# Four rounds of a graph network: the order of the stages in two softmax loops

## The chip, the cores and the metric

One core of one Trainium2 chip runs the kernel. The time is that of the device, in microseconds, for one execution: the kernel before takes 10075.73 us (median of 3 runs, 10074.14 to 10075.74). A smaller number is better. The profile comes from one execution, whose span is 10045.6 us.

## The reference

Four rounds work on 12500 nodes with 64 features and 212500 edges, sorted by the node they end in (`dst`). Each normalises the nodes, sends something along the edges, sums per `dst` and adds the result to the nodes. The change touches the first and the fourth, which both take a softmax over the edges that end in one node:

```python
# round 0 (for each of the 64 features on its own)
m = relu(feats[src] + edge_h) + EPS
gmax = segment_max(m, dst)
ex = exp(m - gmax[dst])
den = segment_sum(ex, dst)
h = segment_sum(m * ex / den[dst], dst)
# round 3 (4 heads of 16 features, 8 relations)
s = leaky_relu(el_all[edge_rel, src] + er_all[edge_rel, dst], 0.2)
m = segment_max(s, dst)
e = exp(s - m[dst])
denom = segment_sum(e, dst)
agg = segment_sum(feat_all[edge_rel, src] * e / denom[dst], dst)
```

Round 1 is a mean over the edges, round 2 a hyperbolic attention. They stay as they are.

## The kernel before, in words

The four edge loops run one after the other, each followed by a part that works on nodes: `softmax_edges(0)` takes about 230 to 2390 us of the span and `softmax_edges(3)` about 7710 to 9880 us.

`softmax_edges` cuts the sorted edges into two halves that are worked on side by side, each half on 64 of the 128 partitions, and takes 512 edges (`W`) of each half in a step: 208 steps (`STEPS`). In a step the edges lie along the free dimension, so the maximum and the sums of a segment can be made by scans along it, which carry their last column on from step to step. Instead of an exponential against the final maximum, the scans use the maximum so far, and the factor `ps_ex` by which the sums so far have to shrink. A step passes through these stages; the letters in brackets are used later:

- GpSimd gathers the rows of `src` by 8 indirect DMAs (L649) into one of four buffers (`SLOTS`). It waits (`rows_read`, the same counter as `turned`) until TensorE has read the step four back.
- SyncE loads the segment marks `part_b` and, for layer 0, the edge attributes, for layer 3 the rows `v_e` and `marks`, also four buffers deep.
- Layer 0: `to_columns` (TensorE, L764 and L766) turns rows and attributes into `ps_score` and adds them; `move` (ScalarE, L824) is the relu. `put_in_bins` (VectorE, L667) and `count` (TensorE, L752) are a histogram that later rounds want; they need nothing of the gathered rows.
- Layer 3: `v_columns` (TensorE, L775) turns `v_e`, `own_values` (VectorE, L676 and L681; OV) makes `own_v` from it, `widen` (ScalarE, L813) spreads the gathered scores over the 16 features of a head, `score_columns` (TensorE, L781 reads `own_v`, L784 reads `wide`, L788 turns the gathered features; SC) makes the scores, `move` (ScalarE, L822; M) copies them.
- `maxima` (VectorE, L688 in layer 3 only, L695, L699, L704, L705, L707; MX): the running maximum and the two differences.
- `exps` (ScalarE, L828 and L829; EX): both exponentials, and the DMA of the maxima (L830).
- `segment_sums` (VectorE, L713, L716, L719; SS): the weighted values and the two running sums.
- `to_rows` (TensorE, L796; TR) turns the sums back, `copy_out` (ScalarE, L836) copies them out of PSUM, `store` (ScalarE's queue, L844) writes them by two DMAs.

Each engine runs its instructions in the order written. That order comes from `written_out`: it is given pairs of a lag and a stage, and for s = 0, 1, 2, ... emits, in the order of the list, each stage for step s minus its lag. Semaphores between the engines are counted per step, so any stage waits until its own inputs are there; `ex`, `weighted`, `ps_ex` and (layer 3) `score_c` exist once, the running `top` and `sums` and `own_v` twice, `ps_score` twice in layer 3 and three times in layer 0.

Of the kernel before, what the change touches and what calls it, by code (L numbers as in the profile page):

```python
# [65 lines left out]
STEPS = CHUNKS // HALVES  # L66
# [10 lines left out]
def build(nc, x, src, dst, edge_attr, edge_type, w0a, b0a, gamma, beta, w0b, b0b, scale0,  # L77
          w1, b1, w2, c2, w3, al3, ar3, b3, out):
    with ExitStack() as whole:
# [448 lines left out]
        def written_out(n, *stages):  # L528

            for s in range(n + max(lag for lag, _ in stages)):  # L530
                for lag, stage in stages:
                    if 0 <= s - lag < n:
                        stage(s - lag, (s - lag) % SLOTS, (s - lag) // SLOTS)

        def softmax_edges(layer):
# [7 lines left out]
            with nc.cleanup_on_exit(), ExitStack() as ctx:  # L543
# [51 lines left out]
                with nc.Block() as block:  # L595
# [60 lines left out]
                    def _(dve):  # L656
# [63 lines left out]
                                                 initial=sums[:, 1 - q, 1, W - 1:W], op0=ALU.mult, op1=ALU.add).then_inc(summed, 1)  # L720

                        if rel:
                            written_out(STEPS, (0, own_values), (3, segment_sums), (2, maxima))
                        else:
                            written_out(STEPS, (0, put_in_bins), (2, segment_sums), (1, maxima))

                        step = stepper(dve, m_step)
                        top_a = top[0:D, END, W:W + 1]
# [17 lines left out]
                    @block.tensor  # L746
                    def _(pe):
                        def count(c, b, r):
                            pe.wait_ge(binned, c + 1)
                            pe.sem_inc(pe_turn, 1)  # L750
                            for t in range(2):
                                mm = nc.tensor.matmul(ps_count[:, t, 0:HOT], ident_b[:, :],  # L752
                                                      hot[:, b % 2, t, :, :].rearrange("p j b -> p (j b)"),
                                                      start=isinstance(c, int) and c == 0,
                                                      stop=isinstance(c, int) and c == STEPS - 1)
                            mm.then_inc(counted, 1)

                        def to_columns(c, b, r):
                            pe.wait_ge(got_edge[b], r * 32 + 32)
                            slot_free(pe, weighed, c, ago=SCORES)  # L760
                            pe.wait_ge(got_rows[b], r * ROWS + ROWS)
                            pe.sem_inc(pe_turn, 1)
                            for k in range(TILES):
                                nc.tensor.matmul(ps_score[:, c % SCORES, k::TILES], rows[:, b, k, :], ident[:, :], start=True, stop=False)  # L764
                                for h in range(HALVES):
                                    mm = nc.tensor.matmul(ps_score[h * D:(h + 1) * D, c % SCORES, k::TILES], attr[:, b, h, k, :],  # L766
                                                          ident[:, :], start=False, stop=True)
                            mm.then_inc(turned, 1)

                        def v_columns(c, b, r):  # L770
                            pe.wait_ge(got_edge[b], r * 48 + 48)
                            slot_free(pe, v_spread, c, ago=1)
                            pe.sem_inc(pe_turn, 1)
                            for k in range(TILES):
                                mm = nc.tensor.transpose(ps_v[:, k::TILES], v_e[:, b, k, :], ident[:, :])  # L775
                            mm.then_inc(v_turned, 1)

                        def score_columns(c, b, r):
                            pe.wait_ge(v_own, c + 1)
                            slot_free(pe, diffed, c)  # L780
                            nc.tensor.matmul(ps_score[:, c % SCORES, :], head_of[:, :], own_v[:, b % 2, :], start=True, stop=False)  # L781
                            pe.wait_ge(widened, c + 1)
                            for k in range(TILES):
                                nc.tensor.matmul(ps_score[:, c % SCORES, k::TILES], wide[:, b % 2, k, :], ident[:, :],  # L784
                                                 start=False, stop=k == TILES - 1)
                            slot_free(pe, weighed, c)
                            for k in range(TILES):
                                mm = nc.tensor.transpose(ps_mult[:, b % 2, k::TILES], rows[:, b, k, HEADS:HEADS + 2 * D], ident[:, :])  # L788
                            mm.then_inc(turned, 1)

                        def to_rows(c, b, r):
                            pe.wait_ge(summed, c + 1)
                            slot_free(pe, copied, c, ago=1)
                            for j in range(2):
                                for k in range(TILES):
                                    mm = nc.tensor.transpose(ps_out[:, j, k * P:(k + 1) * P], sums[:, b % 2, j, k::TILES],  # L796
                                                             ident[:, :])
                            mm.then_inc(back, 1)

                        if rel:  # L800
                            written_out(STEPS, (0, v_columns), (1, score_columns), (3, to_rows))
                        else:
                            written_out(STEPS, (0, to_columns), (1, count), (2, to_rows))

                    @block.scalar
                    def _(act):
                        a = nc.scalar

                        def widen(c, b, r):
                            act.wait_ge(got_rows[b], r * ROWS + ROWS)  # L810
                            slot_free(act, turned, c)
                            for h, at in ((0, 0), (1, HEADS + 2 * D)):
                                ins = a.activation(  # L813
                                    wide[:, b % 2, :, h * D:(h + 1) * D].rearrange("p k (n d) -> p k n d", d=DH),
                                    rows[:, b, :, at:at + HEADS][:, :, :, None].broadcast_to([P, TILES, HEADS, DH]), ACT.Copy)
                            ins.then_inc(widened, 1)

                        def move(c, b, r):
                            act.wait_ge(turned, c + 1)
                            if rel:  # L820
                                slot_free(act, bent, c, ago=1)
                                a.activation(score_c[:, :], ps_score[:, c % SCORES, :], ACT.Copy).then_inc(moved, 1)  # L822
                            else:
                                a.activation(ps_score[:, c % SCORES, :], ps_score[:, c % SCORES, :], ACT.Relu).then_inc(moved, 1)  # L824

                        def exps(c, b, r):
                            act.wait_ge(diffed, c + 1)
                            a.activation(ex[:, :], ex[:, :], ACT.Exp)  # L828
                            a.activation(ps_ex[:, :], ps_ex[:, :], ACT.Exp).then_inc(exped, 1)  # L829
                            act.dma_start(max_b[:, bass.ds(c * W, W)], top[D:P, b % 2, 1:W + 1]).then_inc(put_top[b], 16)  # L830

                        def copy_out(c, b, r):
                            act.wait_ge(back, c + 1)
                            slot_free(act, put[b], r, each=32, ago=1)
                            for j in range(2):
                                ins = a.activation(out_e[:, b, :, :, j * D:(j + 1) * D],  # L836
                                                   ps_out[:, j, :].rearrange("p (k h f) -> p h k f", k=TILES, h=HALVES), ACT.Copy)
                            ins.then_inc(copied, 1)

                        def store(c, b, r):  # L840
                            act.wait_ge(copied, c + 1)
                            act.sem_inc(issue, 1)
                            for h in range(HALVES):
                                act.dma_start(edge_rows(scan_out, c + h * STEPS), out_e[:, b, h, :, :]).then_inc(put[b], 16)  # L844

                        if rel:
                            written_out(STEPS, (0, widen), (1, move), (2, exps), (3, copy_out), (4, store))
                        else:
                            written_out(STEPS, (0, move), (1, exps), (2, copy_out), (3, store))
                        act.wait_ge(parted, 1)  # L850
                        a.activation(apart[:, 0:2], apart[:, 0:2], ACT.Exp).then_inc(powered, 1)

# [1356 lines left out]
```

## Time and profile before

| what | value |
|---|---|
| time, median of 3 | 10075.73 us |
| span of the profiled execution | 10045.6 us |
| TensorE busy | 6609.3 us (66%) |
| VectorE busy | 6940.6 us (69%) |
| ScalarE busy | 4170.6 us (42%) |
| GpSimd busy | 7317.4 us (73%) |
| first and last gather of layer 0 | 232.2 and 2359.4 us |
| first and last gather of layer 3 | 7712.3 and 9839.6 us |

The profile's own execution is 30 us shorter by its span than the median of the timed runs; the span runs from the first instruction to the last, and what lies around it is not in it. An instruction's line is the one in the listing above. Busy shares over the whole span mix four loops and four node parts with different limits, so the rows further down are taken from inside the two softmax loops. TensorE's granted clock is given as a share of 2.4 GHz: 1.00 is that, 0.50 is 1.2 GHz.

### The profile page before, as it was taken

Reading aid. Unit: us, or ns where it says so; the run is one execution under the profiler, and the core shown is the slowest. Engines: PE = TensorE matmul, PEld = TensorE weight load, DVE = VectorE, ACT = ScalarE, POOL = GpSimd, SP = SyncE. Lnnn points to the kernel's source line nnn. Section 1 sums busy time; section 2 is a strip of 40 time slices with the busy share of each in tenths; the row PEclk is TensorE's granted clock in tenths of the full one; section 3 lists DMA queues with packets and bytes.
Section 4 is the critical chain, followed back from the end, with each engine's and each line's share of the span. In section 5 each row is a group of like instructions: output and inputs, shape, how many; then the busy total and the mean of one; then the engine's idle time right before and its main releaser. Section 6 shows DMA issues by size and latency. Waiting matters only on the chain. (4 is left out here: it accounts for less than half of the span.)

```text
span 10045.6 us, 120472 instructions
## 1 busy us (share of the span) xinstructions
PE 6609.3 (66%) x28159; PEld 5230.6 (52%) x28159; DVE 6940.6 (69%) x14143; ACT 4170.6 (42%) x8456; POOL 7317.4 (73%) x7482
## 2 busy tenths in 40 slices
PE   0777777774436566665548888888856776677661
PEld 0444444442235555555448888888854444455441
DVE  4666666666656666663667777777764888888885
ACT  0222222221236666666236666666644333333330
POOL 5777777776477777776877777777756777777775
PEclk9665555565568888888555555555557567655775
DMA  4444444444422222222245555555545444444442
GB/s 99 123 129 129 130 128 130 128 130 78 151 66 66 67 66 66 66 66 62 19 95 106 106 106 106 106 106 106 106 108 150 132 128 132 129 131 129 131 130 72
DMA packets 1318230, 1059.32 MB, mean 105 GB/s; under 512 B 815857, under 2 KB 1034376, under 8 KB 1316531
## 3 DMA queue, kind: packets, MB, share of 16 engines
q0 software_dynamic: 238720, 318.69, 15.9%
q1 hardware_dynamic: 681698, 373.56, 14.5%
q10 hardware_dynamic: 397397, 362.35, 11.0%
q8 instruction: 161, 2.64, 0.1%
q14 instruction: 254, 2.08, 0.1%
HBM read 580.99 MB, written 472.73 MB: 105 GB/s over the span
## 5 line engine op out<-in xcount | busy, mean ns | idle before, releaser
L1173 POOL DMA_INDIRECT h_rows_d<-table,h_idx_d x1840 | 1750.4, 951 | 568.5 <-issue 560.5
L649 POOL DMA_INDIRECT rows<-table,idx_all x1664 | 1621.7, 975 | 527.6 <-issue 506.8
L649 POOL DMA_INDIRECT rows<-table3s,idx_all x1664 | 1621.8, 975 | 518.5 <-issue 506.7
L956 POOL DMA_INDIRECT m_rows<-table,idx_all x1664 | 1572.5, 945 | 507.0 <-issue 507.0
L986 PE MATMUL m_ps_sort<-m_hot_high,m_hot_low 128*128 128x224 f32 x3328 | 936.1, 453 | 621.1 <-DVE m_hot_high L1080 516.0
L986 PEld LDWEIGHTS m_ps_sort<-m_hot_high,m_hot_low 128*128 128x128 f32 x3328 | 822.0, 252 | 706.3 <-DVE m_hot_high L1080 547.6
L1193 PE MATMUL h_ps_sum<-h_rows_d,h_hot 128*128 128x65 f32 x3680 | 818.7, 412 | 324.8 <-DVE h_rows_d L1330 324.8
L764 PE MATMUL ps_score<-ident,rows 128*128 128x128 f32 x1664 | 655.7, 498 | 567.5 <-DMA rows<-table,idx_all 559.2
L1193 PEld LDWEIGHTS h_ps_sum<-h_rows_d,h_hot 128*128 128x128 f32 x3680 | 782.6, 323 | 409.9 <-issue 409.9
L796 PE MATMUL ps_out<-ident,sums 128*128 128x128 f32 x3328 | 714.3, 384 | 281.8 <-DVE sums L719 281.7
L764 PEld LDWEIGHTS ps_score<-ident,rows 128*128 128x128 f32 x1664 | 417.3, 312 | 826.2 <-issue 826.2
L796 PEld LDWEIGHTS ps_out<-ident,sums 128*128 128x128 f32 x3328 | 627.4, 222 | 417.9 <-DVE sums L719 362.0
L1049 DVE TENSOR_TENSOR_SCAN m_sums<-m_same_b,m_sums,m_ps_rows 128x512 f32<-128x512 bf16 x208 | 266.2, 1280 | 826.6 <-issue 637.5
L1211 PE MATMUL h_ps_src<-h_near,h_hot_t 128*128 128x65 f32 x3680 | 829.8, 417 | 2.5 <-ACT h_hot_t L1235 2.5
L1211 PEld LDWEIGHTS h_ps_src<-h_near,h_hot_t 128*128 128x128 f32 x3680 | 809.7, 332 | 3.2 <-issue 3.2
L824 ACT ACTIVATE ps_score<-ps_score 128x512 f32<-128x512 f32 x208 | 121.1, 582 | 1611.4 <-PE ps_score L766 1611.4
L813 ACT ACTIVATE wide<-rows 128x256 f32<-128x256 f32 x416 | 149.9, 407 | 1485.9 <-DMA rows<-table3s,idx_all 1485.9
L1339 DVE SCALAR_TENSOR_TENSOR h_run<-h_run,h_goes_on,h_ps_sum 128x65 f32<-128x65 f32 x1840 | 518.5, 282 | 233.4 <-PE h_ps_sum L1193 5.0
L1024 ACT ACTIVATE m_hot_low<-m_hot_low,record,m_slope 128x128 f32<-128x128 f32 x1664 | 660.0, 480 | 6.1
L667 DVE TENSOR_TENSOR hot<-bins,cat 128x784 bf16<-128x784 bf16 x208 | 202.8, 976 | 647.1 <-PE ps_count L752 647.0
L1088 DVE SCALAR_TENSOR_TENSOR m_junk<-cat,m_ps_base 128x98 f32<-128x98 f32 (+61 forms) x1664 | 586.7, 419 | 0.0
L766 PE MATMUL ps_score<-ident,attr 128*64 128x128 f32 x3328 | 578.0, 448 | 0.0
(425 smaller groups left out, 14380.2 us busy)
## 6 DMA issues: line engine op xcount, KB each, us to landing
scan<-out_e ACTq DMA_DIRECT2D x832, 256.0 KB, 3.2
h_near<-table SPq DMA_DIRECT2D x1840, 32.5 KB
run_g<-h_run ACTq DMA_DIRECT2D x230, 260.0 KB
part_b<-part SPq DMA_DIRECT2D x832, 64.0 KB
max_b<-top ACTq DMA_DIRECT2D x416, 128.0 KB
scan<-m_out_e SPq DMA_DIRECT2D x416, 128.0 KB
attr<-in_edge_attr SPq DMA_DIRECT2D x415, 128.0 KB
h_rows_d<-table,h_idx_d POOLq DMA_INDIRECT x1840
```

What stands on the lines that cost most here:

```text
L649: pool.indirect_dma_start(out=rows[:, b, k, h * GW:(h + 1) * GW], out_offset=None, in_=table3s.rearrange("n (q f) -> (n q) f", f=HEADS) if ...
L764: nc.tensor.matmul(ps_score[:, c % SCORES, k::TILES], rows[:, b, k, :], ident[:, :], start=True, stop=False)
L766: mm = nc.tensor.matmul(ps_score[h * D:(h + 1) * D, c % SCORES, k::TILES], attr[:, b, h, k, :], ident[:, :], start=False, stop=True)
L796: mm = nc.tensor.transpose(ps_out[:, j, k * P:(k + 1) * P], sums[:, b % 2, j, k::TILES], ident[:, :])
L956: pool.indirect_dma_start(out=rows[:, b, k, h * D:(h + 1) * D], out_offset=None, in_=table1, in_offset=bass.IndirectOffsetOnAxis(ap=idx_al ...
L986: nc.tensor.matmul(ps_sort[:, 0:SORTED], hot_low[:, w % 2, j, :], hot_high[:, w % 2, j, :], start=n == 0, stop=n == PC - 1).then_inc(place ...
L1024: ins = a.activation(hot_low[:, w % 2, j, :], hot_low[:, w % 2, j, :], ACT.Relu, bias=record[:, at:at + 1], scale=slope[:, at:at + 1])
L1088: v.scalar_tensor_tensor(junk[:, at % 4, 0:BLOCKS + n], cat[:, p, 0:BLOCKS + n], cat[:, p, BLOCKS + n:BLOCKS + n + 1], ps_base[:, 0:BLOCKS ...
L1173: pool.indirect_dma_start(out=rows_d[:, b, k, :], out_offset=None, in_=table2, in_offset=bass.IndirectOffsetOnAxis(ap=idx_d[:, c * BT + k: ...
L1193: mm = nc.tensor.matmul(ps_sum[:, k // HB, (k % HB) * ACC2:(k % HB + 1) * ACC2], hot[:, b, k, :], rows_d[:, b, k, D + 1:ROW2], start=True, ...
L1211: mm = nc.tensor.matmul(ps_src[:, k // HB, (k % HB) * (D + 1):(k % HB + 1) * (D + 1)], hot_t[:, b % 2, k * P:(k + 1) * P], near[:, b, k, : ...
L1339: v.scalar_tensor_tensor(run[:, b, k, :], before, goes_on[:, bass.ds(c * BT + k, 1)], ps_sum[:, k // HB, (k % HB) * ACC2:(k % HB + 1) * AC ...
```

## The change

The six lists given to `written_out` on VectorE, TensorE and ScalarE (one for each layer) get another order and other lags. No instruction is added or taken away, and no buffer or wait changes. On VectorE `maxima` now comes first, with lag 1, then the stage that needs no gathered rows (`own_values` or `put_in_bins`), then `segment_sums` with lag 1, of the same step as `maxima`. On TensorE `to_rows` follows with lag 2 (layer 3) or 1 (layer 0), ahead of `v_columns` or `count`. On ScalarE `copy_out` and `store` have lag 1 and stand before `exps`, which has lag 0.

```diff
--- before.py
+++ after.py
@@ -720,9 +720,9 @@
                                                  initial=sums[:, 1 - q, 1, W - 1:W], op0=ALU.mult, op1=ALU.add).then_inc(summed, 1)
 
                         if rel:
-                            written_out(STEPS, (0, own_values), (3, segment_sums), (2, maxima))
+                            written_out(STEPS, (1, maxima), (0, own_values), (1, segment_sums))
                         else:
-                            written_out(STEPS, (0, put_in_bins), (2, segment_sums), (1, maxima))
+                            written_out(STEPS, (1, maxima), (0, put_in_bins), (1, segment_sums))
 
                         step = stepper(dve, m_step)
                         top_a = top[0:D, END, W:W + 1]
@@ -798,9 +798,9 @@
                             mm.then_inc(back, 1)
 
                         if rel:
-                            written_out(STEPS, (0, v_columns), (1, score_columns), (3, to_rows))
+                            written_out(STEPS, (1, score_columns), (2, to_rows), (0, v_columns))
                         else:
-                            written_out(STEPS, (0, to_columns), (1, count), (2, to_rows))
+                            written_out(STEPS, (0, to_columns), (1, to_rows), (0, count))
 
                     @block.scalar
                     def _(act):
@@ -844,9 +844,9 @@
                                 act.dma_start(edge_rows(scan_out, c + h * STEPS), out_e[:, b, h, :, :]).then_inc(put[b], 16)
 
                         if rel:
-                            written_out(STEPS, (0, widen), (1, move), (2, exps), (3, copy_out), (4, store))
+                            written_out(STEPS, (0, widen), (0, move), (1, copy_out), (1, store), (0, exps))
                         else:
-                            written_out(STEPS, (0, move), (1, exps), (2, copy_out), (3, store))
+                            written_out(STEPS, (0, move), (1, copy_out), (1, store), (0, exps))
                         act.wait_ge(parted, 1)
                         a.activation(apart[:, 0:2], apart[:, 0:2], ACT.Exp).then_inc(powered, 1)
```

In layer 3 the operations of VectorE follow each other in the same cycle as before; what is different is how many steps lie between them, and that can be read off where the loop begins. VectorE at the start of layer 3 before (L676 and L681 are `own_values`, L688 to L707 `maxima`):

```order
L676 SCALAR_TENSOR_TENSOR spread_v<-marks,spread_v,ps_v 64x512
L681 SCALAR_TENSOR_TENSOR own_v<-marks,rel_of,spread_v 64x512
L676 SCALAR_TENSOR_TENSOR spread_v<-marks,spread_v,ps_v 64x512
L681 SCALAR_TENSOR_TENSOR own_v<-marks,rel_of,spread_v 64x512
L676 SCALAR_TENSOR_TENSOR spread_v<-marks,spread_v,ps_v 64x512
L681 SCALAR_TENSOR_TENSOR own_v<-marks,rel_of,spread_v 64x512
L688 SCALAR_TENSOR_TENSOR ps_score<-ps_score,score_c 128x512
L695 COPY top<-top 128x1
L699 SCALAR_TENSOR_TENSOR top<-part_b,top,ps_score 128x512
L704 TENSOR_TENSOR ps_ex<-top,part_b 128x512
```

And in the changed kernel at the same place:

```order
L676 SCALAR_TENSOR_TENSOR spread_v<-marks,spread_v,ps_v 64x512
L681 SCALAR_TENSOR_TENSOR own_v<-marks,rel_of,spread_v 64x512
L688 SCALAR_TENSOR_TENSOR ps_score<-ps_score,score_c 128x512
L695 COPY top<-top 128x1
L699 SCALAR_TENSOR_TENSOR top<-part_b,top,ps_score 128x512
L704 TENSOR_TENSOR ps_ex<-top,part_b 128x512
L705 TENSOR_TENSOR ex<-ps_score,top 128x512
L707 TENSOR_TENSOR ps_ex<-ps_ex,top 128x512
L676 SCALAR_TENSOR_TENSOR spread_v<-marks,spread_v,ps_v 64x512
L681 SCALAR_TENSOR_TENSOR own_v<-marks,rel_of,spread_v 64x512
L713 TENSOR_TENSOR weighted<-ex,ps_mult 128x512
L716 SCALAR_TENSOR_TENSOR sums<-ps_ex,sums,ex 128x512
```

Before, three steps' `own_values` stand ahead of the first `maxima`; now it is one, and the second `own_values` comes behind the first `maxima`. The first `segment_sums` (L713) follows directly on that.

ScalarE in the middle of layer 3, one step before (L813 `widen`, L822 `move`, L828 to L830 `exps`, L836 `copy_out`, L844 `store`):

```order
L813 ACTIVATE wide<-rows 128x4x64 x2
L822 ACTIVATE score_c<-ps_score 128x512
L828 ACTIVATE ex<-ex 128x512
L829 ACTIVATE ps_ex<-ps_ex 128x512
L830 DMA max_b<-top 64x512
L836 ACTIVATE out_e<-ps_out 128x8x64 x2
L844 DMA scan<-out_e 128x512 x2
```

And changed:

```order
L813 ACTIVATE wide<-rows 128x4x64 x2
L822 ACTIVATE score_c<-ps_score 128x512
L836 ACTIVATE out_e<-ps_out 128x8x64 x2
L844 DMA scan<-out_e 128x512 x2
L828 ACTIVATE ex<-ex 128x512
L829 ACTIVATE ps_ex<-ps_ex 128x512
L830 DMA max_b<-top 64x512
```

`copy_out` and `store` have moved from behind the exponentials to ahead of them.

## Rows read from the trace of the kernel before

**Rows 1.** Page, costliest group: xcount | busy us, mean ns | idle before, released by.

```profile
L649 POOL DMA_INDIRECT rows<-table3s,idx_all x1664 | 1621.8, 975 | 518.5 <-issue 506.7
```

**Rows 2.** Stretch of layer 3; busy us per engine, granted clock, DMA share, GB/s.

```profile
8785.00:9036.00 251.00, 193.61 (x639) 129.03 (x638) 215.02 (x271) 80.17 (x175) 191.29 (x197) 0.50 0.46 131
```

**Rows 3.** Timeline, layer 3, one step: start us, us, engine, line, operation, idle before.

```profile
8904.72 0.67 DVE L688 SCALAR_TENSOR_TENSOR ps_score<-ps_score,score_c 128x512 f32<-128x512 f32 x1
...
8907.96 0.69 DVE L707 TENSOR_TENSOR ps_ex<-ps_ex,top 128x512 f32<-128x512 f32 x1
8908.55 1.26 DVE L676 TENSOR_TENSOR_SCAN spread_v<-marks,spread_v,ps_v 64x512 f32<-64x512 bf16 x1
...
8908.79 2.04 PE L781 MATMUL ps_score<-own_v,head_of 64*128 64x512 f32 x2 [1.09 <-DVE ps_ex L707]
...
8909.85 0.74 DVE L681 SCALAR_TENSOR_TENSOR own_v<-marks,rel_of,spread_v 64x512 f32<-64x512 bf16 x1
...
8910.08 0.40 ACT L813 ACTIVATE wide<-rows 128x256 f32<-128x256 f32 x1
8910.39 0.58 ACT L822 ACTIVATE score_c<-ps_score 128x512 f32<-128x512 f32 x1
...
8910.76 2.08 PE L784 MATMUL ps_score<-ident,wide 128*128 128x128 f32 x8
8910.87 0.62 ACT L828 ACTIVATE ex<-ex 128x512 f32<-128x512 f32 x1
...
8911.39 0.59 ACT L829 ACTIVATE ps_ex<-ps_ex 128x512 f32<-128x512 f32 x1
...
8911.90 1.07 ACT L836 ACTIVATE out_e<-ps_out 128x512 f32<-128x512 f32 x2
8912.01 0.69 DVE L713 TENSOR_TENSOR weighted<-ex,ps_mult 128x512 f32<-128x512 f32 x1 [1.42 <-ACT ps_ex L829]
...
8913.81 1.26 DVE L719 TENSOR_TENSOR_SCAN sums<-ps_ex,sums,weighted 128x512 f32<-128x512 f32 x1
...
8915.12 1.98 PE L796 MATMUL ps_out<-ident,sums 128*128 128x128 f32 x8 [1.25 <-DVE sums L719]
```

**Rows 4.** Timeline, layer 3, its first step and its last.

```profile
7724.88 2.08 PE L784 MATMUL ps_score<-ident,wide 128*128 128x128 f32 x8 [2.51 <-ACT wide L813]
...
7726.75 1.06 PE L788 MATMUL ps_mult<-ident,rows 128*128 128x128 f32 x4
...
9844.10 2.07 PE L784 MATMUL ps_score<-ident,wide 128*128 128x128 f32 x8 [0.70 <-ACT wide L813]
...
9868.03 0.84 ACTq L844 DMA_DIRECT2D scan<-out_e  x2
```

**Rows 5.** Timeline of TensorE in layer 3, a stretch at the upper clock.

```profile
9298.85 1.09 PE L781 MATMUL ps_score<-own_v,head_of 64*128 64x512 f32 x2 [1.09 <-DVE ps_ex L707]
...
9300.69 1.16 PE L784 MATMUL ps_score<-ident,wide 128*128 128x128 f32 x8 [0.75 <-ACT wide L813]
```

**Rows 6.** Timeline of layer 0: one step, and the last store.

```profile
1308.34 0.77 PE L764 MATMUL ps_score<-ident,rows 128*128 128x128 f32 x2 [3.33 <-DMA rows<-table,idx_all]
...
1313.73 0.83 PE L752 MATMUL ps_count<-hot,ident_b 128*128 128x392 bf16 x2
...
1314.36 1.91 PE L796 MATMUL ps_out<-ident,sums 128*128 128x128 f32 x8
...
2369.64 0.58 ACT L824 ACTIVATE ps_score<-ps_score 128x512 f32<-128x512 f32 x1 [8.58 <-PE ps_score L766]
...
2385.00 0.85 ACTq L844 DMA_DIRECT2D scan<-out_e  x2
```

**Rows 7.** Short stretches: busy us per engine, granted clock, DMA share, GB/s.

```profile
8465.60:8468.80 3.20, 2.71 (x12) 2.25 (x12) 3.17 (x6) 0.00 (x0) 2.37 (x3) 0.50 0.15 30
8469.00:8472.20 3.20, 1.60 (x6) 0.81 (x7) 2.79 (x4) 1.29 (x4) 2.37 (x3) 1.00 0.26 46
1311.20:1314.40 3.20, 3.20 (x15) 1.82 (x16) 0.00 (x0) 0.56 (x2) 2.59 (x3) 0.50 0.36 72
```

## The prediction, made before the changed kernel ran

> **What bounds the kernel now.** I read the page's costliest groups first, then the stretches, then the timeline of single steps. The change touches only the two softmax loops, those of layer 0 and layer 3, each of 208 steps. In both the page puts GpSimd's row gathers first: [rows 1] shows the gathers of layer 3, 1664 of them (8 in a step), each 975 ns busy, and of the 518.5 us idle before them 506.7 us "issue", that is GpSimd waiting for nothing. So a step cannot be shorter than 8 x (975 + 305) ns = 10.24 us. The loop does run at that: the first step's L784 starts at 7724.88 and the last one's at 9844.10 [rows 4], and 2119.2 us / 207 = 10.238 us. VectorE is busy for 215 of 251 us there [rows 2], 8.8 us of a step, and waits for the rest; it is not the bound, but only while its work and that of the others need not be done one after the other.
>
> **What the order before hides.** In layer 3 a step c goes through own_values (OV, VectorE L676, L681), score_columns (SC, TensorE L781, L784, L788), move (M, ScalarE L822), maxima (MX, VectorE L688 to L707), exps (EX, ScalarE L828, L829), segment_sums (SS, VectorE L713 to L719), to_rows (TR, TensorE L796), copy_out and store. In the kernel before, VectorE does OV two steps ahead of MX, so SC(c) and M(c) have a step and more to run beside other VectorE work. The cyclic sequence OV, SS, MX stays as it is in the new order; what changes is which step each one works on: MX(c) now stands directly before OV(c+1), and OV(c) directly before SS(c-1), MX(c).
>
> **Layer 3, step by step.** Now MX(c) needs M(c), which needs SC(c), which needs OV(c); and OV(c+1) is queued on VectorE behind MX(c). That closes a ring with one turn for each step. Its terms, with TensorE at its lower clock of 1.2 GHz (granted clock 0.50 in [rows 2]), from [rows 3]:
> - MX: L688 starts at 8904.72, the next operation L676 at 8908.55: 3.83 us
> - OV: 8908.55 to the end of L681 at 8910.59: 2.04 us
> - OV's end to L781: 0.13 us (the same kind of handover: L707 ends at 8908.65, L781 starts at 8908.79)
> - L781 to L784: 8908.79 to 8910.76, 1.97 us
> - L784 and L788: in the first step they follow each other at once, 7724.88 to 7726.75 + 1.06 [rows 4]: 2.93 us
> - handover, M, handover: 0.04 + 0.58 + 0.04 (the handover as from L829's end at 8911.98 to L713 at 8912.01): 0.66 us
>
> Sum 11.56 us, 1.32 us more than the gathers need. While it turns, VectorE idles: after OV it does SS (8912.01 to 8915.07, 3.06 us) and then waits until the 5.69 us of handover, SC and M are over, 2.6 us in every step. What is queued behind that waiting L688 is the rest of MX, the next OV and SS; TensorE's next L781 waits for that OV, and the gathers come to wait for SC, four buffers behind.
>
> The other edits cost nothing beside this ring. ScalarE now does copy_out and store before EX. Counted from the end of SC(c): TR(c-1) 1.98, copy_out 1.07, the two stores' issue 0.84 (9868.03 in [rows 4]) behind a wait for the copies, 0.95, with handovers 4.1 us, and MX(c), with the 0.66 of M and its own 3.93 (L688's start to L707's end), ends at 4.6 us, so EX(c) (L828 at 8910.87 to 8911.98, 1.11 us and a handover of 0.04) is not held up; the cover is 0.4 us. Past it EX only ends later, and it has 0.9 us before SS(c) feels that, since SS(c) stands behind OV(c+1) (2.04) while EX takes 1.15; and SS itself has the 2.6 us of idling before the ring would grow. Widening the rows (L813, two of 0.40) follows EX and is ready before L781 ends. v_columns behind TR is ready 1.4 us before OV asks. No DMA is added or removed; SP's queue waits for MX and OV of four steps back, as before.
>
> **The clock.** Three terms of the ring are TensorE's. At its upper clock (2.4 GHz) L781 takes 1.09 us and the eight of L784 1.16 us [rows 5], against 1.97 and 1.8; with L788 at a bit over half, the ring would be about 9.6 us, under 10.24. So both ends of the unknown are 11.56 (no gain from the clock) and 10.24 (gathers bound again). Which? In the new order TensorE's work comes as one burst (L781, L784, L788, TR, v_columns, 7.9 us at the lower clock) and an idle stretch of about 3.6 us, and the ring's terms are the burst's first 4.9 us. The nearest pattern in this trace is layer 0, where a step is also one burst: L764 at 1308.34 to the count at 1313.73 and TR at 1314.36 [rows 6]; in the stretch 1311.20 to 1314.40, fully busy, the clock is still 0.50 [rows 7]. So a burst begins at the lower clock and gets the upper one late or not at all. I take a ring of 11.4 us: the lower clock, less a tenth or two for steps in which L781 begins before the clock has fallen.
>
> In rows, transposes count for the clock: from 8465.60 to 8468.80 TensorE ran only the transposes L796 and L775, 2.71 us busy at 0.50, and from 8469.00 on it had 1.00 [rows 7]. The Trainium skill says otherwise (TensorE: Matmul & The Clock Gate, Part 4: PE-mode transpose): a transpose does not count as busy and does not bring the full clock. By that rule the burst's second half would never raise it and the ring would stay at 11.56 us, 33 us more for the kernel than by my value; the trace disagrees with it.
>
> **Layer 0.** There MX(c) does not feed anything that its own next step needs on TensorE, so no such ring exists. From the arrival of a step's rows: to_columns 5.4 us (1308.34 to 1313.73), then TR of the step before 2.0, then the count 0.8: 8.2 us. SS of the step before must be over 5.4 us after the arrival. It starts when EX ends: TR 7.4, copy_out 8.5, store 9.5, EX 10.7, SS 13.7 us after the arrival before, which is 3.5 us after this one: 1.9 us to spare. The ring SS, TR, copy_out, store, EX is 3.06 + 1.98 + 1.07 + 0.95 + 1.15 and handovers, 8.5 us, below 10.24. Cost 0 in the steady state.
>
> **Both ends.** With smaller lags the pipelines drain sooner. Layer 3 before: from the last L784 (9844.10) to the end of the last store's issue (9868.87) 24.8 us [rows 4]; now SC 2.93 + M 0.66 + MX 3.93 + EX 1.19 + SS 3.10 + TR 2.0 + copy_out and store 2.1 = 15.9 us, 8.9 us less. Layer 0 before: from M at 2369.64 to 2385.85 [rows 6], 16.2 us; now 0.6 + 3.3 + 1.2 + 3.1 + 2.0 + 2.1 = 12.3 us, 3.9 us less. Together -12.8 us.
>
> **Sum.** 207 x (11.40 - 10.238) = +240.5 us; with -12.8 it is +227.7 us. The profiled execution's span is 10045.6 us, so the changed one's would be 10273 us; the 30 us between the span and the median of 10075.73 I keep, which gives 10303 us.
>
> **The rivals.**
> - The clock closes the ring (not slower). If L781, L784 and L788 run mostly at 2.4 GHz, the ring is 9.6 us and the gathers bound again; only the drains are left: 10075.7 - 12.8 = 10063 us. It decides from a ring of 10.24 us, that is when about two thirds of the 1.95 us between 11.56 and 9.6 are won. For it: in layer 3 of before there are stretches with L781 at 1.09 us [rows 5]. Against: those come where short pieces of TensorE work are spread over the step; the burst pattern of layer 0 starts low. 6 in 100.
> - Half way: L781 has the upper clock in most steps, L784 and L788 are not. The ring is 11.56 - 0.9 = 10.7 us, the kernel 10063 + 207 x 0.43 = 10152 us; with everything up to 11.1 us, 10240 us. For it: before, an L781 at the upper clock is common [rows 5]. Against: TensorE had then idled 1.09 us before it, now it idles 3.6 us. 16 in 100.
> - Layer 0 closes too: if TR before the count holds up to_columns of the next step, layer 0 loses as much as layer 3, 10303 + 240 = 10540 us. Against: the 1.9 us to spare. 2 in 100.
> - The edit moves nothing, since the cyclic sequence on VectorE is the same. The rows of the order at the loop's start, in the section on the change, show that OV now runs one step ahead of MX's and no more. Under 1 in 100, and it would give 10076 us.
>
> **How the numbers follow.** The forecast, a ring of 11.1 to 11.75 us, has 76 in 100: 10240 to 10376 us. The range leaves out the ring at the upper clock and half of the half-way case below, and rings above 11.65 us above: 10190 to 10355 us. This kernel's measurement tells 0.2%, 20 us, from no change; slower by more than that needs a ring over 10.4 us: 0.92. Within it are the ring at the upper clock and the unmoved kernel: 0.07. Faster by over 20 us would need more than both drains: 0.01.
>
> **What would show it.** Layer 3: L784 every 11.4 us; VectorE idle 2.6 us before L688, released by ScalarE's score_c L822; gathers no longer back to back but idle for the transposed rows; L781 released by own_v L681; the last L784 near 10085 us after the span's start. Layer 0: still 10.24 us a step, its last store 4 us earlier. It is wrong if L784's spacing stays at 10.24 us, or if L688's wait is for something else than L822.

## The result and the profile after

The changed kernel takes 10333.1 us (median of 4 runs, 10329.47 to 10335.4), the kernel before 10075.74 us beside it: 1.0256 times as long, 95% interval 1.0244 to 1.0268, that is 257 us slower. The forecast was 10303 us, with a range to 10355 us.

The timeline of the changed kernel in layer 3, one turn of the ring, answers to [rows 3]:

```profile
9012.35 0.70 DVE L688 SCALAR_TENSOR_TENSOR ps_score<-ps_score,score_c 128x512 f32<-128x512 f32 x1 [2.69 <-ACT score_c L822]
...
9016.21 1.26 DVE L676 TENSOR_TENSOR_SCAN spread_v<-marks,spread_v,ps_v 64x512 f32<-64x512 bf16 x1
...
9017.51 0.74 DVE L681 SCALAR_TENSOR_TENSOR own_v<-marks,rel_of,spread_v 64x512 f32<-64x512 bf16 x1
...
9018.31 2.07 PE L781 MATMUL ps_score<-own_v,head_of 64*128 64x512 f32 x2 [4.06 <-DVE own_v L681]
...
9020.31 2.07 PE L784 MATMUL ps_score<-ident,wide 128*128 128x128 f32 x8
...
9022.17 1.06 PE L788 MATMUL ps_mult<-ident,rows 128*128 128x128 f32 x4
...
9023.27 0.60 ACT L822 ACTIVATE score_c<-ps_score 128x512 f32<-128x512 f32 x1 [5.19 <-PE ps_mult L788]
...
9023.90 0.70 DVE L688 SCALAR_TENSOR_TENSOR ps_score<-ps_score,score_c 128x512 f32<-128x512 f32 x1 [2.69 <-ACT score_c L822]
```

From L688 to L688 are 11.55 us, and each stage begins within some hundredths of a us where the one above ends: MX 3.86, OV 2.04, handover 0.06, L781 2.00, L784 and L788 2.92, handover, M and handover 0.67. VectorE waits 2.69 us before L688, for the L822 that was forecast, and TensorE's L781 waits for own_v. Before, L781 was released by the maxima and SS by the exponentials [rows 3].

The page's groups of the gathers, layer 3 and layer 0 (layer 3 of before is [rows 1]):

```profile
L649 POOL DMA_INDIRECT rows<-table3s,idx_all x1664 | 1664.0, 1000 | 714.4 <-issue 452.8
...
L649 POOL DMA_INDIRECT rows<-table,idx_all x1664 | 1634.3, 982 | 527.6 <-issue 506.9
```

Layer 3's gathers now idle 714 us, 196 us more than before, and most of the new idling ends with L788. Layer 0's never wait, as before, yet they are busy 13 us longer; more on that below. The first and the last L784 of layer 3, its last store, and M and the last store of layer 0, which answer to [rows 4] and [rows 6]:

```profile
2383.14 0.58 ACT L824 ACTIVATE ps_score<-ps_score 128x512 f32<-128x512 f32 x1 [7.58 <-PE ps_score L766]
...
2394.57 0.82 ACTq L844 DMA_DIRECT2D scan<-out_e  x2
...
7752.41 2.08 PE L784 MATMUL ps_score<-ident,wide 128*128 128x128 f32 x8 [3.75 <-ACT wide L813]
...
10138.31 2.07 PE L784 MATMUL ps_score<-ident,wide 128*128 128x128 f32 x8
...
10153.14 0.82 ACTq L844 DMA_DIRECT2D scan<-out_e  x2
```

(10138.31 - 7752.41) / 207 = 11.526 us a step against 10.238: +266.7 us. The drains take 15.65 us (forecast 15.9) and 12.25 us (forecast 12.3). 266.7 - 9.1 - 3.9 = 253.7 us, of 257 measured. The traces themselves differ by more, 284 us, since this one has everything ahead of layer 3 27.5 us later (L784 at 7752.41 for 7724.88): layer 0's gathers take 13 us more and its drain 4 us less, and 14 us are in round 2's gathers, which the change does not touch (L1173, 1764.6 us in all for 1750.4). The other 4 or so are spread. So single traces differ by some 15 us for other reasons than the change.

Stretches of the changed kernel (busy us on TensorE, its weight loads, VectorE, ScalarE, GpSimd, then granted clock, DMA share, GB/s); the first answers to [rows 2]:

```profile
8785.00:9036.00 251.00, 150.02 (x572) 109.86 (x572) 190.97 (x239) 74.65 (x153) 175.12 (x175) 0.67 0.44 116
...
9010.80:9014.20 3.40, 3.40 (x17) 2.88 (x15) 1.85 (x3) 1.37 (x3) 1.88 (x2) 0.50 0.15 21
9014.30:9017.60 3.30, 0.00 (x0) 0.00 (x0) 3.23 (x6) 1.48 (x4) 2.54 (x3) 1.00 0.59 180
9017.80:9021.00 3.20, 2.69 (x5) 1.19 (x6) 3.20 (x4) 0.28 (x1) 2.50 (x3) 0.50 0.67 192
```

The mean clock is higher than before (0.67 for 0.50) and does not help the ring: it is at 2.4 GHz from 9014.30 to 9017.60, while TensorE does nothing, and back at 1.2 GHz when the ring needs L781. In many steps it has risen already for the end of the burst (the turn before has the four v_columns transposes, L775, in 0.60 us for 1.06), but these are not in the ring either. L781 takes 2.03 us or more in every one of the 208 steps.

### The profile page after: what moved, and what is told of

The parts are those of the page before. It is cut to its first block and busy times, and to the rows that moved or that the text cites. A ratio compares the mean times of both kernels' runs of the same rounds, so it can differ in the third digit from the quotient of the medians.

```text
span 10329.8 us, 120472 instructions
## 1 busy us (share of the span) xinstructions
PE 6579.1 (64%) x28159; PEld 5287.3 (51%) x28159; DVE 6968.4 (67%) x14143; ACT 4235.9 (41%) x8456; POOL 7386.8 (72%) x7482
## 3 DMA queue, kind: packets, MB, share of 16 engines
q10 hardware_dynamic: 397397, 362.35, 10.6%
## 5 line engine op out<-in xcount | busy, mean ns | idle before, releaser
L649 POOL DMA_INDIRECT rows<-table3s,idx_all x1664 | 1664.0, 1000 | 714.4 <-issue 452.8
L1173 POOL DMA_INDIRECT h_rows_d<-table,h_idx_d x1840 | 1764.6, 959 | 569.4 <-issue 560.6
L649 POOL DMA_INDIRECT rows<-table,idx_all x1664 | 1634.3, 982 | 527.6 <-issue 506.9
L781 PE MATMUL ps_score<-own_v,head_of 64*128 64x512 f32 x416 | 430.6, 1137 | 974.8 <-DVE own_v L681 974.8
L764 PE MATMUL ps_score<-ident,rows 128*128 128x128 f32 x1664 | 634.8, 483 | 553.4 <-DMA rows<-table,idx_all 429.6
L796 PE MATMUL ps_out<-ident,sums 128*128 128x128 f32 x3328 | 736.1, 395 | 20.0 <-DVE sums L719 20.0
L836 ACT ACTIVATE out_e<-ps_out 128x512 f32<-128x512 f32 x832 | 451.5, 594 | 447.3 <-PE ps_out L796 447.3
L781 PEld LDWEIGHTS ps_score<-own_v,head_of 64*128 64x128 f32 x416 | 103.3, 307 | 1036.1 <-DVE own_v L681 1036.1
```

The lines of the kernel that those rows point to most:

```text
L649: pool.indirect_dma_start(out=rows[:, b, k, h * GW:(h + 1) * GW], out_offset=None, in_=table3s.rearrange("n (q f) -> (n q) f", f=HEADS) if ...
L1173: pool.indirect_dma_start(out=rows_d[:, b, k, :], out_offset=None, in_=table2, in_offset=bass.IndirectOffsetOnAxis(ap=idx_d[:, c * BT + k: ...
```

## The experiments

Ratios and differences are to the kernel before on the same chip, whose median was 10052.8 us beside e1 to e4, 10068.7 us beside e5 to e8 and 10068.8 us beside e9 to e12. The expectations were reckoned from its 10075.7 us, so it is their differences that are compared and not their absolute times.

### One layer at a time

e1: the new lists only in layer 3. 

> The new lists in layer 3 alone, layer 0 as before. Ring theory (OV, SC, M, MX of one step in a row, 11.53 us at the lower clock): L784 every 11.53 us, 207 x 1.29 = +267 us, drain -9, in all about 10334 us. Rival, layer 0 carries part of the loss (in the changed kernel's trace its gathers took 13 us more): 10320 us or less.

e2: only in layer 0. 

> The new lists in layer 0 alone. Ring theory: no ring in layer 0, the gathers bind at 10.24 us a step, only the drain is 3.9 us shorter: 10072 us. Rival, the new order makes the gathers of layer 0 slower, as the +13 us of the trace could be read: about 10085 to 10089 us.

```diff
# e1                                        (e2: the other branch of each)
-  if rel: written_out(STEPS, (0, own_values), (3, segment_sums), (2, maxima))
+  if rel: written_out(STEPS, (1, maxima), (0, own_values), (1, segment_sums))
...
```

e1: 10308.4 us, 1.0255 (1.0239 to 1.0271), +255.6 us for 258 expected, as much as the whole loss. e2: 10076.3 us, 1.0025 (1.0015 to 1.0034), +23 us: not the 4 us less that was expected, but the rival, and about twice the 9 to 13 us that it gave. The two together are 279 us, 22 more than the changed kernel loses; with intervals of 16 and 10 us on them and 12 us on the changed kernel, that does not tell how much layer 0 costs beside layer 3. Layer 0's gathers in e2, and below in e1, where layer 0 is as before (before itself has 1621.7, 975):

```profile
L649 POOL DMA_INDIRECT rows<-table,idx_all x1664 | 1648.4, 991 | 527.6 <-issue 506.8
```

```profile
L649 POOL DMA_INDIRECT rows<-table,idx_all x1664 | 1623.4, 976 | 527.6 <-issue 506.9
```

The 25 us are in the gathers' own duration; the idling between them is equal.

### Opening the ring

e3: a step more between OV and MX, order within the lists as in the changed kernel. 

> Changed kernel, but in layer 3 maxima and segment_sums lag 2 instead of 1 (to_rows, copy_out, store 3, move 1, exps 2), so that own_values is again one step ahead of maxima; the order within the lists as in the changed kernel. Ring theory: back to 10.24 us a step, drains 4 and some 3 us shorter than before: about 10068 us. Rival, the loss comes from the order within the step (maxima directly ahead of own_values, copy_out and store ahead of the exponentials): it stays at 10300 us or more.

```diff
-  (1, maxima), (0, own_values), (1, segment_sums)
+  (2, maxima), (0, own_values), (2, segment_sums)
-  (1, score_columns), (2, to_rows), (0, v_columns)
+  (1, score_columns), (3, to_rows), (0, v_columns)
-  (0, widen), (0, move), (1, copy_out), (1, store), (0, exps)
+  (0, widen), (1, move), (3, copy_out), (3, store), (2, exps)
```

e4: the small lags kept, own_values and v_columns put first. 

> Changed kernel, layer 3 only edited: lists start with own_values on VectorE and v_columns on TensorE, lags unchanged (0, 1, 1 and 0, 1, 2). OV(c+1) then runs before MX(c) and SC(c+1) beside it. Ring theory: the longest ring left is VectorE's own OV, MX, handover and EX, SS, 2.04 + 3.93 + 1.2 + 3.1 = 10.2 to 10.3 us, just at the gathers' 10.24; about 10065 us, at most 10080. Rival, the small lags as such (one step between gather and sums) are what costs: over 10200 us.

```diff
-  (1, maxima), (0, own_values), (1, segment_sums)
+  (0, own_values), (1, maxima), (1, segment_sums)
-  (1, score_columns), (2, to_rows), (0, v_columns)
+  (0, v_columns), (1, score_columns), (2, to_rows)
```

e3: 10061.5 us, 1.0009 (1.0000 to 1.0018). e4: 10028.1 us, 0.9974 (0.9964 to 0.9984). e3 is 9 us slower than the kernel before, e4 25 us faster; 8 and 11 us faster were expected. Layer 0, changed in both, costs what e2 shows, and what is left of layer 3's loss is nothing. e3 keeps the order within the lists and e4 the small lags, so it is the ring and neither of these. e4 gains more than expected: its gathers of layer 3 (the row below) take 950 ns each, not the 975 of [rows 1], and L784 comes every 10.04 us, so 10.24 us was no floor.

```profile
L649 POOL DMA_INDIRECT rows<-table3s,idx_all x1664 | 1580.8, 950 | 518.1 <-issue 506.7
```

e9: as e4, but v_columns stays behind score_columns. 

> As e4 (own_values first), but v_columns stands behind score_columns on TensorE. That closes another ring: EX, widen (0.75), L784 and L788 (2.93), v_columns (1.06), OV (2.04), MX (3.93) and handovers, 12.1 us a step at the lower clock, 1.9 us over the gathers: about 10450 us, slower than the changed kernel. Rival, any order with own_values first is free: about 10030 us.

```diff
-  (0, v_columns), (1, score_columns), (2, to_rows)
+  (1, score_columns), (0, v_columns), (2, to_rows)
```

One run: 10345.6 us, 277 us over the kernel before. A loss of 374 us was expected and a gain of 46 by the rival, so the loss is there at three quarters of its size. The other ring is in its trace:

```profile
9000.13 0.69 DVE L688 SCALAR_TENSOR_TENSOR ps_score<-ps_score,score_c 128x512 f32<-128x512 f32 x1
...
9005.15 0.70 ACT L813 ACTIVATE wide<-rows 128x256 f32<-128x256 f32 x2
...
9005.90 2.08 PE L784 MATMUL ps_score<-ident,wide 128*128 128x128 f32 x8 [4.52 <-ACT wide L813]
...
9007.77 1.06 PE L788 MATMUL ps_mult<-ident,rows 128*128 128x128 f32 x4
9008.62 1.06 PE L775 MATMUL ps_v<-ident,v_e 128*64 128x128 f32 x4
...
9009.77 1.27 DVE L676 TENSOR_TENSOR_SCAN spread_v<-marks,spread_v,ps_v 64x512 f32<-64x512 bf16 x1 [1.47 <-issue]
...
9011.75 0.68 DVE L688 SCALAR_TENSOR_TENSOR ps_score<-ps_score,score_c 128x512 f32<-128x512 f32 x1
```

It turns in 11.62 us here (11.58 on average, from the first L784 to the last), not 12.1; 207 x 0.5 us is the 100 us by which the forecast was too long. The sum of the expectation was half a microsecond too long: it added full durations where the next operation of the same engine starts before the last is over (L788 at 9007.77 to L775 at 9008.62 is 0.85 for a duration of 1.06; L813 starts 0.07 before L829 has ended).

### Terms in the ring and beside it

e5: L788 out of the ring. 

> Changed kernel; in score_columns of layer 3 the transposes L788 (ps_mult) move from behind the score matmuls to ahead of the wait for own_v, into TensorE's idle stretch. Ring theory: L788 with its 1.06 us, less the 0.2 us by which L784's end is seen later than the start of the next, leaves the ring: 11.53 - 0.9 = 10.6 us, 10335 - 190 = about 10145 us. Rival, the loss is not this ring: no change at 10333 us.

```diff
 def score_columns(c, b, r):
+    pe.wait_ge(got_rows[b], r * ROWS + ROWS)
+    slot_free(pe, weighed, c)
+    for k in range(TILES): transpose(ps_mult[...], rows[...], ident)    # L788
     pe.wait_ge(v_own, c + 1)
 ...
```

e6: exponentials first on ScalarE. 

> Changed kernel; on ScalarE in layer 3 the exponentials stand ahead of copy_out and store again, all lags as in the changed kernel. Ring theory: neither is in the ring, same time, 10333 us within 10. Rival, putting copy_out and store ahead of the exponentials is part of the loss: faster by 50 us or more.

```diff
-  (0, widen), (0, move), (1, copy_out), (1, store), (0, exps)
+  (0, widen), (0, move), (0, exps), (1, copy_out), (1, store)
```

e6: 10336.2 us, 1.0268 (1.0251 to 1.0286), as the changed kernel: copy_out and store ahead of the exponentials are free, as forecast. e5: 10070.6 us, 1.0002 (0.9992 to 1.0011), 2 us over the kernel before where 69 were expected. TensorE in e5, where L785 is the old L781, L788 the old L784, L782 the moved transposes:

```profile
9005.61 0.60 PE L782 MATMUL ps_mult<-ident,rows 128*128 128x128 f32 x4
9010.71 1.34 PE L785 MATMUL ps_score<-own_v,head_of 64*128 64x512 f32 x2 [4.50 <-DVE own_v L681]
9011.98 2.08 PE L788 MATMUL ps_score<-ident,wide 128*128 128x128 f32 x8
```

In this step the first matmuls of the burst take 1.34 us for 2.07: the clock is still at 2.4 GHz when they begin. That is so in about half of the steps (under 1.5 us in 47% of them). Without L788 the ring would be 10.6 us; in this turn, with what the clock gives, it is 10.1 (9000.61 to 9010.71), and on average L788 comes every 10.25 us, which is the gathers' pace again. The edit took a term away and, by moving it, changed the phase of the clock; the run does not separate the two shares.

### The clock by itself

e7: 12 useless transposes in TensorE's idle stretch. 

> Changed kernel plus useless work: in layer 3 TensorE does 12 extra transposes of ident into the score bank (overwritten by L781) in its idle stretch, before the wait for own_v: 12 x 0.22 = 2.7 us at the lower clock, of 3.6 us idle. If TensorE's work counts for the clock and the clock is what makes the ring 11.53 and not 9.6: the clock stays at 2.4 GHz, the gathers bind at 10.24 us, and the kernel gets faster by up to 265 us, about 10070 us. By the rule that transposes do not count as activity: no change, 10333 us, or somewhat more where they delay L781.

e8: 6 useless matmuls. 

> The same with 6 ordinary matmuls of ident with ident (two passes each, about the same 2.7 us) in place of the 12 transposes. Clock theory, and also by the rule for matmuls: about 10070 us. If it is as slow as 10333 us, the clock does not follow TensorE's work in that stretch or is not what the ring hangs on.

```diff
 def score_columns(c, b, r):
-    pe.wait_ge(v_own, c + 1)
     slot_free(pe, diffed, c)
+    for k in range(12): transpose(ps_score[:, c % SCORES, 0:P], ident, ident)   # e8: 6 x matmul
+    pe.wait_ge(v_own, c + 1)
```

e7: 10069.4 us, 1.0000 (0.9990 to 1.0010). e8: 10068.8 us, 1.0002 (0.9992 to 1.0011). Work that nobody needs takes the changed kernel's whole loss away (267 us, by e6 on the same chip). In e7:

```profile
8785.00:9036.00 251.00, 170.72 (x933) 135.41 (x932) 217.81 (x274) 85.27 (x174) 191.28 (x197) 0.84 0.49 131
```

```profile
9005.16 1.12 PE L783 MATMUL ps_score<-own_v,head_of 64*128 64x512 f32 x2 [2.66 <-DVE own_v L681]
9006.21 1.16 PE L786 MATMUL ps_score<-ident,wide 128*128 128x128 f32 x8
```

The mean clock is 0.84, and in this step the ring's matmuls take 1.12 and 1.16 us. That holds for two steps in three (L783 under 1.5 us in 66% of them, 2.07 at most in the others); it is enough, with four buffers between, for the gathers to bind again: a step takes 10.25 us. Transposes do it as well as matmuls. The Trainium skill's rule that a transpose does not count as busy (TensorE: Matmul & The Clock Gate, Part 4: PE-mode transpose) does not hold here: by it e7 would have stayed at 10333 us. The changed kernel by itself did not tell the two apart: its 11.53 us a step are close to the 11.56 us that the prediction gives by that rule. Its clock did rise behind every burst, though, only not for the ring's terms, and that is what e7 and e8 change.

### Layer 0's gathers

e11: each result of layer 0 stored twice. 

> Layer 0 alone changed (as e2), and in layer 0 each result is stored twice (the second time into a buffer that is not read before it is overwritten). If the transfers of the stores lengthen the gathers that run beside them: the gathers of layer 0 take clearly more than e2's 1648 us, 1670 or more, and the kernel loses as much. Rival, the long gathers have nothing to do with the stores: 1648 us within 5.

e12: store behind the exponentials. 

> Layer 0 alone changed (as e2), but store stands behind the exponentials, so that its DMAs start some 1.5 to 2 us later in the step; no wait is in a ring. If the phase of the stores against the gathers is what costs: the gathers of layer 0 change by 10 us or more from e2's 1648 us, in either direction. Rival, the phase does not matter: within 5 us.

```diff
 # e11, in store(); the counts for put double with it (64 for 32)
+    if not rel: act.dma_start(edge_rows(scan3, c + h * STEPS), out_e[:, b, h, :, :]).then_inc(put[b], 16)
 # e12
-  (0, move), (1, copy_out), (1, store), (0, exps)
+  (0, move), (1, copy_out), (0, exps), (1, store)
```

e11: 10087.7 us, 1.0018 (1.0008 to 1.0028), +19 us; layer 0's gathers take 1641.4 us, 7 less than e2's 1648 and outside either expectation, but far from 1670: twice the bytes stored do not lengthen them. e12: 10075.2 us, 1.0006 (0.9997 to 1.0016), +6 us, gathers 1635.9 us. That is 12 us less than e2, but the same order of layer 0 has 1634.3 us in the changed kernel and 1659.4 in e4, so this one trace decides nothing. All traces with the new order of layer 0 lie between 1634 and 1659 us, the three with the old one (before, e1, e10) at 1622 to 1625. So the order costs, by longer gathers, some 10 to 35 us of them, and the mass of the stores is not why.

The traces on record say more than these two runs. Most gathers take 0.94 us; those over 0.96 us start while VectorE is at work on one of three instructions. Two steps show it, the changed kernel's and e4's, both in layer 3:

```profile
9014.40 0.70 DVE L704 TENSOR_TENSOR ps_ex<-top,part_b 128x512 f32<-128x512 f32 x1
9014.45 1.46 POOL L649 DMA_INDIRECT rows<-table3s,idx_all  x1 [0.30 <-issue]
```

```profile
9000.53 0.70 DVE L704 TENSOR_TENSOR ps_ex<-top,part_b 128x512 f32<-128x512 f32 x1
9001.04 0.99 POOL L649 DMA_INDIRECT rows<-table3s,idx_all  x1 [0.32 <-issue]
```

Both gathers end 0.8 us after L704 does, so the one that starts early in L704 is long and the one that starts near its end hardly so. Over the softmax loops of all 14 traces 5378 of 46592 gathers take over 0.96 us, and 5321 of these start while VectorE runs L704, L681 (layer 3) or L667 (layer 0), and end 0.80 to 0.84 us after it; of the gathers that start at other times only 57 of 38505 are long. These three are the instructions of the loops whose two tensor inputs both lie in SBUF. With the new order of layer 0, 187 to 205 of its 1664 gathers are long, with the old one 119 to 125. So what the order changes is how gathers fall on these instructions. This is read from traces and not tested: no run moved one of the three alone.

### The version that beats both

e10: layer 0 as before, layer 3 as in e4. 

> Layer 0 as before, layer 3 with own_values and v_columns first (as in e4). If the two parts add up (layer 0's new order costs 23 us alone, layer 3's variant gained 25 us beside it): 45 us less than before, about 0.4 to 0.5% faster. Rival, the 23 and 25 us come from something that differs from kernel to kernel as a whole: no better than e4 (25 us, 0.25%).

10013.9 us, 0.9946 (0.9933 to 0.9960): 55 us less than before and the fastest of all; 45 were expected. The two parts add up (23 and 25 us), within what the intervals tell. Its gathers, layer 3 and layer 0:

```profile
L649 POOL DMA_INDIRECT rows<-table3s,idx_all x1664 | 1583.1, 951 | 518.7 <-issue 506.8
...
L649 POOL DMA_INDIRECT rows<-table,idx_all x1664 | 1625.4, 977 | 527.6 <-issue 506.8
```

## Why the prediction was right, and where it was off

- What bounds: right that the gathers bind in both loops before, with 8.8 us of VectorE in a step of 10.24. Wrong that 10.24 us is what a step cannot go below. The 975 ns of [rows 1] is a mean over gathers of 944 ns and about one longer one in a step. How long that one is depends on where it falls on VectorE's L704 or L681: 1.19 us on average before, 1.01 us in e10, whose mean is 951 ns. Its step in layer 3 is 8 x (951 + 305) ns = 10.05 us.
- The ring: right in its members, its terms and its place. Forecast 11.56 us at the lower clock, measured 11.53; e3 and e4 open it and the loss is gone, e1 shows that layer 3 alone loses 256 us.
- The clock: the step that was mis-sized. I gave the ring "a tenth or two" back (11.40) since L781 might begin before the clock has fallen. It gave back nothing: the clock is up behind the ring's terms and in the idle stretch, and down again before L781 in every step (2.03 us or more in all 208). 207 x 0.126 = 26 us, which is nearly all of the 30 us by which the forecast was short. e7 and e8 show that the first rival, the clock closing the ring, hung on the clock alone, as said: it comes true when TensorE is kept at work.
- Layer 0: no ring, right (its gathers never wait). "Cost 0 in the steady state" was wrong: e2 loses 23 us, with gathers 27 us longer than before. The changed kernel's trace has 13 us of that, so its last store of layer 0 comes 9.5 us later and not 4 us earlier. The term was put at nothing because only waits and rings were looked at, and the gathers' duration was taken as fixed.
- ScalarE's new order is free: right (e6). The drains: right within 0.3 us.
- The 30 us between span and median was taken as something around the span. In the changed kernel the profiled run took 10331.5 us with a span of 10329.8, so that is 1.7 us; the other 28 us must be a difference between executions, though the time of the one that was profiled before is not on record. It did not change the forecast, which only kept it.

## What to carry to other kernels

When a list of stages is reordered, write down for each engine which step each stage works on and look for rings: a chain through several engines that comes back to the same engine one step later. If its sum is more than the bound so far, the sum is what a step costs, whatever the busy shares say; take each term from start to start (11.56 us forecast so, 11.53 measured; 12.1 by full durations in e9, 11.6 measured). One stage moved ahead of the ring's entry opens it (e4). And price TensorE's terms at the clock that it will have when they begin: here that was 1.2 GHz in every step behind 4.7 us of idling (the median before L781), and 2.4 GHz in two steps of three once that stretch was filled (e7).

## What was not expected of the hardware

Useless work made the kernel faster: 12 transposes a step (e7) took it from 1.0256 to 1.0000 times the kernel before. And GpSimd's gathers are not of constant length: for 1664 of them in layer 0, where they wait for nobody, 1622 to 1625 us with one order of the other engines and 1634 to 1659 with another; in layer 3 from 1581 us (e4) to 1666 us (e1). The long ones are those that start while VectorE works on an instruction with two tensor inputs in SBUF, and they end some 0.8 us after it. What passes between the two engines there the traces do not show.
